# Attention and expert layers on one core: how the split query and key parts are stored, counted and made

## The reference, cut to what matters

```python
x = x + _layernorm(attn(_layernorm(x)))     # attention, causal, 16 heads of 8
x = x + _layernorm(ffn(_layernorm(x)))      # 7 routed experts (top 2) and a shared one

qkv = (x @ w_qkv).reshape(Bx, Tx, 3, H, HD) # B 2, T 1024, H 16, HD 8
scores = jnp.einsum('bhqd,bhkd->bhqk', q, k) * SCALE
...                                          # causal mask
geo_bias = q_proj[..., :, None] * k_proj[..., None, :]
scores = scores + head_scales[None, :, None, None] * geo_bias
attn = jax.nn.softmax(scores, axis=-1)
out = jnp.einsum('bhqk,bhkd->bhqd', attn, v)
```

## Time and profile before

| | before |
|---|---|
| time, median of 3 runs (lowest to highest) | 480.75 us (479.73 to 484.54) |
| the profiled execution | 477.46 us, span 475.7 us |
| mean granted TensorE clock | 0.931 of full speed |
| busy share of the span: PE, DVE, ACT, POOL | 87%, 68%, 55%, 37% |
| data moved | 46.57 MB, mean 98 GB/s |

### The profile page before, as it was taken

The page is one execution under the profiler, slowest core; times in us unless marked ns, Lnnn a source line. Parts: engine busy times, 40 slices in busy tenths (PEclk is TensorE's granted clock), DMA queues, the critical chain, the costliest instruction groups (busy, mean ns, idle before and its releaser), DMA issues. The chain is left out here.

```text
span 475.7 us, 10729 instructions
## 1 busy us (share of the span) xinstructions
PE 413.5 (87%) x3820; PEld 240.9 (51%) x3820; DVE 322.9 (68%) x1116; ACT 259.4 (55%) x465; POOL 175.1 (37%) x325
## 2 busy tenths in 40 slices
PE   1846899889999999999999878988999999999870
PEld 0521224223233233233343263655799999999870
DVE  2977869979999999999865928498333333333242
ACT  1530458347887887887986628552334443444223
POOL 5000135303123123114263425333766767673302
PEclk9995569869999999999999979999999999999986
DMA  4076112440021122000000044100687788877142
GB/s 116 1 222 177 34 39 78 125 121 16 1 70 37 35 69 65 6 2 4 4 2 3 1 129 137 44 2 1 188 242 240 229 238 234 243 239 233 36 167 88
DMA packets 39031, 46.57 MB, mean 98 GB/s; under 512 B 5635, under 2 KB 26500, under 8 KB 38980
## 3 DMA queue, kind: packets, MB, share of 16 engines
q1 hardware_dynamic: 34820, 39.34, 27.9%
q0 software_dynamic: 2432, 4.99, 3.7%
q10 hardware_dynamic: 1728, 1.57, 1.1%
HBM read 34.80 MB, written 10.88 MB: 96 GB/s over the span
## 5 line engine op out<-in xcount | busy, mean ns | idle before, releaser
L712 ACT ACTIVATE probs<-banks 128x1024 f32<-128x1024 f32 (+1 forms) x192 | 153.0, 812 | 47.6 <-PE banks L553 29.8
L539 PE MATMUL banks<-k_st,q_st 48*128 48x512 bf16 (+3 forms) x384 | 111.9, 358 | 16.4 <-DMA k_st<-k_rows 8.8
L831 DVE CUSTOM_DVE_ANT_0 masked<-banks,mask_max 128x512 bf16<-128x512 f32 (+3 forms) x256 | 110.5, 487 | 17.3 <-PE banks L539 15.9
L553 PE MATMUL banks<-q_st,k_st 51*128 51x512 bf16 (+3 forms) x384 | 100.8, 344 | 4.6 <-DMA q_st<-mx_rows 2.7
L581 PE MATMUL banks<-probs,v_ones 128*9 128x128 f32 (+3 forms) x1536 | 97.7, 340 | 0.6 <-POOL probs L447 0.5
L539 PEld LDWEIGHTS banks<-k_st,q_st 48*128 48x128 bf16 x384 | 31.8, 95 | 101.2 <-DVE mx_part L834 32.3
L834 DVE TENSOR_REDUCE mx_part<-banks 128x1 f32<-128x512 f32 x128 | 77.8, 682 | 3.6 <-PE banks L539 3.3
L447 POOL TENSOR_SCALAR_AFFINE_SELECT probs<-probs 128x256 f32<-128x256 f32 x128 | 52.4, 415 | 64.4 <-ACT probs L712 31.9
L1615 DVE TENSOR_TENSOR hidden<-banks,gate 128x512 f32<-128x512 f32 x38 | 26.3, 692 | 66.4 <-PE banks L1253 64.9
L433 POOL CAST mx_split<-mx 128x16 bf16<-128x16 f32 x16 | 3.1, 196 | 125.9 <-DVE mx L837 75.8
L1128 POOL DMA_INDIRECT results<-result,target x38 | 37.4, 983 | 30.4 <-DVE result L1623 30.4
(11 more groups left out here) (197 smaller groups left out, 473.1 us busy)
## 6 DMA issues: line engine op xcount, KB each, us to landing
w_g<-in_w_gate SPq DMA_DIRECT2D x38, 256.0 KB, 3.3
w_u<-in_w_up SPq DMA_DIRECT2D x38, 256.0 KB, 4.4
q_st<-q_rows SPq DMA_DIRECT2D x32, 96.0 KB, 2.3
k_st<-k_rows SPq DMA_DIRECT2D x32, 96.0 KB, 2.3
q_rows<-parts SPq DMA_DIRECT2D x18, 128.0 KB, 2.4
k_rows<-parts SPq DMA_DIRECT2D x18, 128.0 KB, 2.4
w_d<-in_w_down SPq DMA_DIRECT2D x8, 256.0 KB, 4.5
back<-results SPq DMA_DIRECT2D x4, 512.0 KB, 5.8
```

The source lines that it names most:

```text
L539: nc.tensor.matmul(max_bank[e % RING][:, 0:width], q_st[g][rows, c, p, (i % CH) * P:(i % CH + 1) * P], k_st[g][rows, kc, p, 0:width], star ...
L553: last = nc.tensor.matmul(dst[a][:, 0:BANK - first], k_st[g][rows, j // CH, p, (j % CH) * P:(j % CH + 1) * P], q_st[g][rows, c, p, first:B ...
L712: last = nc.scalar.activation(probs[s % PROBS][:, 2 * p:2 * p + 2, first:BANK], slot_pair[at % 2].rearrange("p (a t) -> p a t", a=2)[:, :, ...
L831: nc.vector.tensor_tensor_reduce(masked[e % RING][:, 0:width], src, mask_max[:, BANK - width:], 1.0, NEG, ALU.add, ALU.max, accum_out=dst) ...
```

## The change

Four things change, all in the first stage.

- **Transfers with a repeating source.** The row order of a stack becomes channel by channel: row `d * 6 + combo` where it was `combo * 8 + d`. A part that a stack holds several times at equal steps is stored by one transfer whose source repeats the part with a step of zero. `COPIES` lists them for the query (3) and the key (4): part, first row, step and count. Twelve transfers of a half become seven; `STORES` is that seven.
- **Query and key counted apart.** `parts_ready` rises after each low part, so twice a half, and SP stores the query's copies before it waits for the key's.
- **The last half, `LATE`** (batch 1, half 1), is not split by VectorE. ACT copies its query and key from PSUM whole, in 32 bits, to `late` (memory of `x2_t`), and GpSimd makes the three parts from there in four operations each: `split_late(0)` ahead of the attention loop, `split_late(1)` behind the maxima rows of item 0.
- PE's wait ahead of the loop becomes six counts of `parts_ready` and both of `late_taken`; SP's stores of the last half wait for `late_ready`.

```diff
+COPIES = (((0, 0, 1, 3), (1, 3, 1, 2), (2, 5, 1, 1)), ((0, 0, 1, 1), (0, 3, 2, 2), (1, 1, 3, 2), (2, 2, 1, 1)))
+STORES = sum(len(x) for x in COPIES)
+LATE = (B - 1, 1)
+        late = x2_t[:, 0:2 * CH, :].rearrange("c (i t) p -> c i (t p)", i=2)

+        def store_copies(queue, b, half, qk):
+
+            for part, first, step, count in COPIES[qk]:
+                copies = (q_rows, k_rows)[qk][b * H:(b + 1) * H, :, half * BANK:(half + 1) * BANK].rearrange(
+                    "h (d r) t -> (h d) r t", d=HD)
+                queue.dma_start(copies[:, first:first + step * (count - 1) + 1:step, :],
+                                parts[b][:, half, qk, part, :].unsqueeze(1).broadcast_to([P, count, BANK])
+                                ).then_inc(parts_stored[b * 2 + half], 16)

             def store_parts(b, half):
-                sp.wait_ge(parts_ready, b * 2 + half + 1)
-                for qk, dst in ((0, q_rows), (1, k_rows)):
-                    for row, combo in enumerate(COMBOS):
-                        sp.dma_start(
-                            dst[b * H:(b + 1) * H, row * HD:(row + 1) * HD, half * BANK:(half + 1) * BANK],
-                            parts[b][:, half, qk, combo[qk], :]).then_inc(parts_stored[b * 2 + half], 16)
+                for qk in range(2):
+                    if (b, half) == LATE:
+                        sp.wait_ge(late_ready, qk + 1)
+                    else:
+                        sp.wait_ge(parts_ready, (b * 2 + half) * 2 + qk + 1)
+                    store_copies(sp, b, half, qk)

             def load_stacks(b, r, c):
-                sp.wait_ge(parts_stored[b * 2 + c], 16 * 2 * len(COMBOS))
+                sp.wait_ge(parts_stored[b * 2 + c], 16 * STORES)

+            def split_late(qk):
+
+                b, half = LATE
+                high, mid, low = (parts[b][:, half, qk, i, :] for i in range(3))
+                left = late[:, qk, :]
+                pool.wait_ge(late_taken, qk + 1)
+                nc.gpsimd.tensor_copy(high, left).then_inc(late_steps, 1)
+                pool.wait_ge(late_steps, 3 * qk + 1)
+                nc.gpsimd.tensor_tensor(left, left, high, ALU.subtract).then_inc(late_steps, 1)
+                pool.wait_ge(late_steps, 3 * qk + 2)
+                nc.gpsimd.tensor_copy(mid, left).then_inc(late_steps, 1)
+                pool.wait_ge(late_steps, 3 * qk + 3)
+                nc.gpsimd.tensor_tensor(low, left, mid, ALU.subtract).then_inc(late_ready, 1)

+            split_late(0)
             done = 0
             for s, m in STEPS:
...
                 if m is not None and m + 1 == item_end(done):
                     split_rows(done)
                     done += 1
+                    if done == 1:
+                        split_late(1)

-                        pe.wait_ge(parts_ready, done - 1)
+                        pe.wait_ge(parts_ready, 2 * (done - 1))

-            pe.wait_ge(parts_ready, 4)
+            pe.wait_ge(parts_ready, 6)
+            pe.wait_ge(late_taken, 2)

                     act.wait_ge(q_projected, b * 2 + half + 1)
-                    nc.scalar.activation(parts[b][:, half, 0, 0, :], bq, ACT.Copy).then_inc(high_ready, 1)
+                    if (b, half) == LATE:
+                        nc.scalar.activation(late[:, 0, :], bq, ACT.Copy).then_inc(late_taken, 1)
+                    else:
+                        nc.scalar.activation(parts[b][:, half, 0, 0, :], bq, ACT.Copy).then_inc(high_ready, 1)
...
-            act.wait_ge(parts_ready, 2)
-            for qk, dst in ((0, q_rows), (1, k_rows)):
-                for row, combo in enumerate(COMBOS):
-                    act.dma_start(dst[0:H, row * HD:(row + 1) * HD, BANK:2 * BANK], parts[0][:, 1, qk, combo[qk], :]
-                                  ).then_inc(parts_stored[1], 16)
+            act.wait_ge(parts_ready, 4)
+            for qk in range(2):
+                store_copies(act, 0, 1, qk)

                 for half in range(2):
+                    if (b, half) == LATE:
+                        continue
                     for qk in range(2):
...
-                        last = nc.vector.tensor_tensor(low, left, mid, ALU.subtract)
-                    last.then_inc(parts_ready, 1)
+                        nc.vector.tensor_tensor(low, left, mid, ALU.subtract).then_inc(parts_ready, 1)
```

More of the change, by code:

```diff
@@ L310, in program @@
         parts_ready = sem("parts_ready")
+        late_taken = sem("late_taken")
+        late_steps = sem("late_steps")
+        late_ready = sem("late_ready")
         parts_stored = [sem(f"parts_stored{i}") for i in range(2 * B)]
@@ L688, in _ @@
                     act.wait_ge(q_projected, b * 2 + half + 1)
-                    nc.scalar.activation(parts[b][:, half, 0, 0, :], bq, ACT.Copy).then_inc(high_ready, 1)
+                    if (b, half) == LATE:
+                        nc.scalar.activation(late[:, 0, :], bq, ACT.Copy).then_inc(late_taken, 1)
+                    else:
+                        nc.scalar.activation(parts[b][:, half, 0, 0, :], bq, ACT.Copy).then_inc(high_ready, 1)
                     act.wait_ge(k_projected, b * 2 + half + 1)
-                    nc.scalar.activation(parts[b][:, half, 1, 0, :], bk, ACT.Copy).then_inc(high_ready, 1)
+                    if (b, half) == LATE:
+                        nc.scalar.activation(late[:, 1, :], bk, ACT.Copy).then_inc(late_taken, 1)
+                    else:
+                        nc.scalar.activation(parts[b][:, half, 1, 0, :], bk, ACT.Copy).then_inc(high_ready, 1)
                     act.wait_ge(v_projected, b * 2 + half + 1)
```

## The result

The changed kernel takes **473.12 us** (median of 20 runs, 471.04 to 481.33), the kernel before 479.88 beside it (20 runs, 477.35 to 488.71). The ratio is 0.9845 with a 95% interval of 0.9814 to 0.9876: 7.4 us faster, 1.5%. The profiled execution took 473.17 us, with a span of 471.4 (before: 477.46 and 475.7).

What follows compares the result with a forecast made beforehand. It took the store-and-read-back chain, paced by store issue, to bound the first stage. Earlier, fewer stores and quicker loads move TensorE's first maxima from 38.20 to 32.4; 5.8 us off the 480.75 median gives 475.0 us, range 471.0 to 479.5.

Steps and rivals of the forecast that it cites:

- Counting apart: SP's first store: issues at about 21.05 instead of 22.84, once the query part is split, gaining 1.79 us.
- landing time: First stack's loads: last issued at 29.69, landing 2.7 us later at 32.4, bounds 31.8 and 34.5.
- Seven stores for twelve: SP's first-half stores: 3.7 us of issue, transfer binds with 5.26 us at 299 GB/s; SP goes on at 28.26, not 32.71.
- rival 4: First-half stores: merged transfers move at a fraction of the rate; at 100 GB/s the kernel takes 486.8 us; chance 0.05.
- VectorE's gate: TensorE's wait before the first maxima: six parts done at 29.97 instead of 33.55, so the load at 32.4 stays last.
- GpSimd's side: GpSimd's splits: four operations at 1.27 us, 5.1 us each split, under 9.3 us of cover, so cost 0.
- One for one to the end: From TensorE's first maxima to the kernel's end: the 5.8 us earlier start reaches the end whole.
- 1: First-half stores: pieces, not issues, set the pace; only 1.8 us won, TensorE at 36.4, 479.0 us; chance 0.15.
- 2: Attention part: the clock returns 7 us later in the moved schedule, 3 us go back, 478.0 us; chance 0.12.
- 3: Maxima through item 1: the clock holds 2.4 GHz, at least 2.7 us more won, 472.3 us; chance 0.08.

Runs made afterwards that it cites:

- twelve stores in the new order: Changed kernel with every row set stored by its own transfer again, twelve per half, keeping the new row order: 473.55 us, ratio 0.9852 to the kernel before.
- Order alone: Kernel before with only its stores' row order changed to the new one, nothing merged: 477.38 us, ratio 0.9919 to the kernel before.
- twelve transfers in the old order: Changed kernel with the kernel before's twelve stores per half and row order, counting apart and GpSimd's split kept: 478.93 us, ratio 0.9934 to the kernel before.
- loads held: Changed kernel with SP holding the first stack loads until GpSimd has split the last half's query part: 483.97 us, ratio 1.0044 to the kernel before.
- stores by halves: Changed kernel with both GpSimd splits behind item 0's rows and the first half stored and loaded in two sets of 8 heads: 481.78 us, ratio 0.9944.
- the repeated changed kernel: Changed kernel run again unaltered, beside the kernel before in another group of runs: 475.58 us, ratio 0.9882 to the kernel before.

## Why the prediction was right, point by point

It said 475.0 us within 471.0 to 479.5, faster likelier than not; 473.12 was measured. The place (the gap ahead of the first maxima), the chain of stores and loads and the releaser were as forecast; why the stores became quicker was not. That the number came so close is in part luck: the start moved by 7.0 us where 5.8 was forecast, but at equal clock only 4.3 to 5.5 of it reached the end, where the prediction let all of it through. The parts:

- **Counting apart, 1.79 us.** First store at 21.25 for 21.05, the 0.2 us being the later start of the profile. Taken back, it cost 3.1 us at the start of the maxima, not 1.8: the prediction knew that the loads get ahead of ACT's stores by it, but priced that only in the landing time.
- **Seven stores for twelve.** Issue 0.53 each was taken, and 0.53 (query) to 0.58 (key) measured. The step that failed is the rate: 299 GB/s was taken, the best mixed row of before, and 322 to 354 ran, so 1.573 MB took 4.7 us, not 5.26. What stands around the data, the start of the first store and the tail of the last, took 1.4 us (6.07 from the first store to the first load, less 4.7), not 1.95. So the first load left at 27.32, not 28.26: 0.9 of the 1.2 us by which TensorE beat the forecast (31.23 for 32.4); the loads gave the other 0.2 (the last is issued 1.3 us after the first, for 1.43, and lands after 2.6, for 2.7). The rows behind the 299 were of the old form: with twelve stores in the new order the engines moved 264 GB/s at a share of 0.80, before 202 at 0.73; per full share that is 330 against 277, so the order made not only the issue but also the transfer cheaper.
- **What made it cheap** was wrong. The prediction read 0.648 us as the price of an issue and saved it by having fewer. It was the price of one form of transfer, 16x8x512; with the rows in an order that lets the destination be 128x512, an issue takes 0.475. Order alone takes 3.6 us off the start, merging 1.1 us more on top of order, counting and split. The prediction mentioned the order only as a danger (rival 4); that it pays was not seen. The rule of the Trainium skill it weighed ("DMA: Bandwidth & Descriptors", section "Issuing engines are not separate DMA queues"), that sequencer time is usually small relative to the DMA, does not hold for these 128 KB stores in either form: with twelve of them the share stays at 0.65 to 0.83, whichever order, and only merged does it reach 1.
- **VectorE's gate** was put at 29.97 and stood at 30.98. No contention was taken, by the masked maximum, which indeed never slowed (0.69 at 40.60, in the middle of GpSimd's second split). The operation that did slow is the subtraction with both inputs in SBUF, by 0.83 us; it cost nothing only because the load came 0.25 us later. The Trainium skill says in "SBUF — State Buffer", section "Who interferes with whom", that a VectorE instruction with two SBUF inputs contends with a GpSimd instruction that reads SBUF. The trace agrees: the subtraction, counted back 0.69 us from its end, began at about 30.3, near the end of GpSimd's own (30.44). The rule names the operation that slowed; a bound for it stood in the prediction's own row of one GpSimd operation, 1.27 us.
- **GpSimd's side.** 1.27 us per operation was taken, 0.61 (cast) and 1.15 to 1.22 (subtraction) measured. The second split fills 39.52 to 43.27, and GpSimd still waits 2.26 us for VectorE behind it. Cost 0, as forecast:

```profile
42.12 1.15 POOL L451 TENSOR_TENSOR parts<-x_t,parts 128x512 bf16<-128x512 f32 x1
45.54 0.20 POOL L463 CAST mx_split<-mx 128x16 bf16<-128x16 f32 x1 [2.26 <-DVE mx L870]
```

- **One for one to the end.** 5.8 us at the gate was to be 5.8 in the time. It was 7.0 at the gate, and 7.4 by the ratio; but at equal clock 4.3 (up to 5.5 with the lean of the line taken out), the rest being fewer microseconds at 1.2 GHz. Over the kernels of the table a microsecond of earlier start goes with 0.6 to 0.9 at equal clock, and with 0.3 for twelve transfers in the old order; the kernel with its loads held (0.4 us of start) and the one with stores by halves, which waits again later, are left out. In the profiled execution the first load behind the attention is issued 7.4 us earlier (271.20 for 278.64) and the span is 4.3 shorter: 1.3 us go between there and the first expert load, 1.9 behind it, where TensorE waits 1.1 us for `w_u` and 1.7 more for `back`. The profile of the repeated changed kernel shows neither of these two waits, so they need not come with the change; there the first load behind the attention is issued 5.5 us earlier than before (273.17) and the span is 4.6 shorter.
- **Rivals.** 1 and 4 fell with the share of 1.0 at 350 GB/s: six copies in three transfers were issued in 1.58 us, in six transfers in 2.77, and a repeating source behind a leading dimension of 128 loses no rate. 2 fell in the form it had: the clock rose 14.8 us after the first score (62.3) where it rose 14.1 us after it before (68.8). 3 fell too: the clock dropped at 35.0, in the midst of the maxima. Windows of the changed kernel around both:

```profile
34.00:35.00 1.00, 0.57 (x3) 0.18 (x2) 1.00 (x5) 0.00 (x0) 0.00 (x0) 1.00 1.02 346
35.00:36.00 1.00, 0.78 (x3) 0.20 (x2) 1.00 (x5) 0.00 (x0) 0.00 (x0) 0.51 1.12 378
...
62.00:63.00 1.00, 0.84 (x7) 0.25 (x4) 0.98 (x5) 0.84 (x2) 0.11 (x1) 0.84 0.00 0
```

Still, the clock is what spreads the runs. In the profiled execution with twelve transfers in the new order it came back only in the 76th microsecond, item 1 took 12.35 us and item 2 10.43 (10.48 and 7.67 in the changed kernel), so 4.6 us of the gain went that way in that execution:

```profile
74.00:75.00 1.00, 1.00 (x19) 0.47 (x20) 0.55 (x4) 0.88 (x2) 0.00 (x0) 0.50 0.00 0
75.00:76.00 1.00, 0.65 (x6) 0.15 (x6) 0.59 (x3) 1.00 (x3) 0.41 (x1) 0.91 0.00 0
```

**What stays open.** Kernels whose maxima start by 32.4 us have a median of 65 to 73 us at 1.2 GHz (81 with the stores by halves, where TensorE waits another 6 us up to 44), those that start later 72 to 88. Whether an early start itself brings the clock back sooner, or the few executions of each happen to lie so, these runs don't settle. Nor is it shown what in the form 16x8x512 makes its issue dear, or what merging would give in the old order, which no run tried.

## What to carry to other kernels

When transfers are issued at a steady pace and the DMA engines are not full, look at the form of one transfer before counting how many there are: an order in DRAM that lets 128 partitions be the leading dimension took a quarter off each issue here, for nothing. Price an operation that is given to GpSimd also by what VectorE does beside it, by the kind of its operands and not by its length. And where the granted clock varies between executions, compare kernels at equal clock before reading a few us out of medians.

## What the runs showed of the hardware

- On SP a store of 128 KB is issued in 0.64 to 0.65 us where its DRAM side is 16x8x512, and in 0.475 where it is 128x512; the seven merged ones, of one to three copies, take 0.53 to 0.58 on average.
- A source repeated with the partitions in front moved at 322 to 354 GB/s, above the 299 of the best row of stores and loads before. That need not be the repetition's doing: with twelve stores that repeat nothing, a window of ACT's stores and the loads reached 365.
- Transfers from 64 partitions ran at 186 to 201 GB/s with the DMA engines 87 to 96% busy. The Trainium skill, "SBUF — State Buffer", section "Can I just issue two DMAs to hit both halves?", says that only a transfer over all 128 partitions reaches all ports; these rows agree.
- A 128x512 subtraction of VectorE with both inputs in SBUF went from 0.69 to 1.52 us beside a GpSimd subtraction, and GpSimd's cast behind it from 0.61 to 0.95; VectorE's masked maximum, which reads PSUM, did not change.
